# Where the cross-attention mask is added: from ScalarE and TensorE to VectorE in the maximum pass, from TensorE to ScalarE in the second

## The chip, the cores and the metric

The kernel runs on one core of one Trainium2 chip. The metric is the time of one execution on the device in microseconds (us).

## The reference, cut to what matters

A decoder layer over 16 sequences of 256 tokens of width 256: a delta-rule attention block, a cross attention, and a feed-forward block with fake quantization, each behind a layer norm and with a residual. The change touches only the scores of the cross attention, which has 16 heads of width 16 and one mask of 256 x 256 for all sequences and heads:

```
q, k, v = layernorm(x) @ Wq.T, ctx @ Wk.T, ctx @ Wv.T            # split into 16 heads
scores  = q @ k.T / sqrt(16), masked where mask == 0             # [16 sequences, 16 heads, 256, 256]
x       = x + (softmax(scores) @ v) @ Wo.T
```

## The kernel before, in words

The kernel has four phases: `phase_a` (projections and short convolutions), `phase_b` (long convolution and early inverses), `phase_cx` (the rest of the first attention, gates, and the cross attention) and `phase_f` (the feed-forward block). The change lies wholly in `phase_cx`.

`phase_cx` is a software pipeline over the 16 sequences. A hand-written list, `C_ORDER` (L789), names some 250 steps with a stage number. A *turn* goes through this list once; in turn n, a step of stage s works on sequence n - s. Each engine walks the same list and executes its own steps strictly in that order, waiting on semaphores. Five streams of work are so interleaved: stages 0 to 3 of the first attention and its gates, stage 3 of the cross attention's projections, stage 4 its maximum pass, stage 5 its second pass, stages 6 to 8 its output, layer norm and store.

**The maximum pass (stage 4)** finds for each query and head the largest masked score, so that the exponential can be shifted. It has 16 steps (k = 0 to 15), each for one half of the queries and two heads, 128 x 512 scores in the one PSUM bank `psA`:

- `kA` (ScalarE, L1694 to L1701) writes the mask, held twice side by side in `mask_q` as bf16, into `psA` and waits before that for the maximum of step k - 1.
- `sA` (TensorE, L1416 to L1435) waits for the mask and adds the scores of two heads with two matmuls of 96 x 256 that accumulate (`start=False`). Where `masked_by_act` (L1082) is false (the very first step and all of the last sequence) TensorE adds the mask itself, by a matmul of the mask with the identity (L1429).
- `mA` (VectorE, L2134 to L2140) takes both maxima with one `tensor_reduce` of 128 x 512.

After `mA15`, `maxT`, `sh1`, `sh2` and `ld_S` (L1436, L1680, L2141, L1152) turn the maxima, split them into two bf16 rows and store them as two more rows of the stacked queries `Qs`; the second pass subtracts them inside the score matmul.

**The second pass (stage 5)** has 16 steps too, one for each head, 128 x 512 transposed scores (keys by queries) in the one bank `psB`:

- `sB` (TensorE, L1442 to L1459) waits for the exponential of step k - 1 (`pexp_ready`), then writes the mask into the bank by a matmul with the identity (L1454, 512 columns), then adds the scores with two matmuls of 98 x 256 (L1457).
- `eB` (ScalarE, L1693) takes the exponential of the bank into `PT`.
- `pv` (TensorE, L1471) multiplies four heads at a time with V.

The last sequence alternates two banks in the maximum pass and the last two sequences do so in the second pass (`bank_A`, `bank_B`, L1086 and L1091).

Steps of other streams that the prediction names: `proj` and `x1` (L1375, L2079) the first attention's output and residual; `statx`, `rstdx`, `xnx`, `xT`, `xTc`, `qproj`, `qhigh`, `qrest`, `qlow` (L1886, GpSimd, L2131, L1414, L1678, L1397, L1665, L2116, L1861) the layer norm and the query projection, split into three bf16 parts; `ostat` (GpSimd, from L1808), `st8` (L2066), `oT8` (TensorE, L1342) statistics for the output gate; `stats` (GpSimd, from L1772) and `st16` (L1977) those of the kind gates; `w5` (L1556) and `maxT` (L1440), which share a PSUM bank; `xd` (L1551), `OT0` (L1708); `prepare_weights` (L1891), the feed-forward weights' quantization, spread over the `mA` steps of sequence 14.

The mask is prepared once, at `st8` of sequence 0 (L2061), and turned by TensorE into `mask_k` for the second pass.

Of the kernel before, what the change touches and what calls it, by code (L numbers as in the profile page):

```python
# [5 lines left out]
BF16 = mybir.dt.bfloat16  # L6
INT8 = mybir.dt.int8
INT32 = mybir.dt.int32
ALU = mybir.AluOpType
# [739 lines left out]
def weights_T(shared):  # L749
# [39 lines left out]
C_ORDER = [(0, "tt"), (3, "og2"), (3, "oge"), (1, "rv"), (4, "kA1"), (3, "ogs"), (3, "ctxT"), (2, "tT"), (2, "tTc"), (3, "cTc"),  # L789
# [23 lines left out]


def phase_cx(nc, sems, dram, keep, ident, used, early):
    with ExitStack() as ctx:
# [181 lines left out]
        mask_q = xb("mask_q", [P, TT, 2, L], BF16)  # L998
# [83 lines left out]
        def masked_by_act(b, k):  # L1082

            return b < B - 1 and b + k > 0
# [111 lines left out]
        def _(pe):  # L1196
            pe.wait_ge(S_zero, 3)

            def part(op, b):
# [130 lines left out]
                elif op == "oT8":  # L1330
# [3 lines left out]
                    if b == 0:  # L1334

                        pe.wait_ge(prep_step, 6)
                        for t in range(TT):
                            for k in range(TT):
                                nc.tensor.transpose(ps_e_bf[:, 2 * L + k * L + t * P:2 * L + k * L + (t + 1) * P],
                                                    mask_q[:, t, 0, k * P:(k + 1) * P], ident_bf[:])  # L1340
# [75 lines left out]
                elif op[:2] == "sA":  # L1416
# [7 lines left out]
                    if masked_by_act(b, k):  # L1424
                        pe.wait_ge(mask_written, HEAD_STEPS * b + k)
                    else:
                        if b + k > 0:
                            pe.wait_ge(maxed, HEAD_STEPS * b + k - two)
                        nc.tensor.matmul(bank.rearrange("p t q -> p (t q)"), ident_bf[:],  # L1429
                                         mask_q[:, t].rearrange("p s k -> p (s k)"), start=True, stop=False, skip_group_check=True)  # L1430
                    for s in range(2):
                        h = 2 * pair + s
                        last = nc.tensor.matmul(bank[:, s], Qs[slot][0:S_ROWS, h, t * P:(t + 1) * P], Ks[slot][0:S_ROWS, h],  # L1433
                                                start=False, stop=True, skip_group_check=True)
# [7 lines left out]
                elif op[:2] == "sB":  # L1442
# [9 lines left out]
                    if b + k > 0:  # L1452
                        pe.wait_ge(pexp_ready, HEAD_STEPS * b + k - two)
                    nc.tensor.matmul(bank.rearrange("p t q -> p (t q)"), ident_bf[:], mask_k[:].rearrange("p t q -> p (t q)"),  # L1454
# [71 lines left out]
        def _(act):  # L1526
            act.wait_ge(V_set, 1)

            def part(op, b):
# [164 lines left out]
                elif op[:2] == "kA":  # L1694
                    k = int(op[2:])
                    if masked_by_act(b, k):
                        if b == 0 and k == 1:
                            act.wait_ge(prep_step, 6)
# [866 lines left out]
```

## Time and profile before

| what | us |
|---|---|
| median of 3 runs | 1311.63 (1310.03 to 1312.18) |
| the profiled execution's own time | 1311.31 |
| its span in the trace | 1309.5 |
| busy: TensorE, its weight loads | 1086.7, 801.0 |
| busy: VectorE, ScalarE, GpSimd | 958.1, 877.4, 639.4 |

The profiled execution took 1.81 us more than its span. "Busy" counts compute instructions alone; PE is TensorE, PEld its weight loads, DVE VectorE, ACT ScalarE, POOL GpSimd, SP the queue of the DMAs. PEclk is the clock that TensorE was granted, as a share of 2.4 GHz. Matmuls overlap: what one costs the queue is the step from its start to the next one's, not its length. The same holds for VectorE, by some 0.08 us for each instruction. A releaser in brackets is the instruction whose end let a waiting one start. `phase_cx` takes turns of equal length from 481 us on; the turn of 713.0 to 759.6 us stands for them.

### The profile page before, as it was taken

What the parts mean: (1) busy time and instruction counts of PE and PEld (TensorE: products, weight loads), DVE (VectorE), ACT (ScalarE), POOL (GpSimd) and SP (SyncE); (2) the same over time, 40 slices, a digit from 0 to 9 for tenths busy, and PEclk for the clock granted to TensorE, in tenths of its full rate; (3) what the DMA queues carried; (4) which work ended last, traced back from release to release, by engine and by line L of the source; (5) the groups of instructions that cost most, each with busy time, mean ns of one, the idle gap of its engine ahead of it and who ended that gap; (6) DMA issues with size and microseconds to landing.
All of it is one profiled execution on the core that took longest, in us unless ns stands there. A gap on an engine that the chain in (4) does not pass through costs nothing. (4 is left out here: it accounts for less than half of the span.)

```text
span 1309.5 us, 27566 instructions
## 1 busy us (share of the span) xinstructions
PE 1086.7 (83%) x8643; PEld 801.0 (61%) x8643; DVE 958.1 (73%) x2188; ACT 877.4 (67%) x1695; POOL 639.4 (49%) x2360
## 2 busy tenths in 40 slices
PE   5988887685777779999999999999999887876756
PEld 4766666584555556776776676676677655443225
DVE  4988898687666766777877877787787566634985
ACT  4777787432343467878878878887887665444866
POOL 4777775404265355465465556546546643111006
PEclk9988999795566789999999999999999988996989
DMA  5766666546115133333434343343342341205007
GB/s 166 219 186 205 208 198 203 185 88 168 57 57 153 52 103 110 118 100 105 147 110 120 119 122 123 110 135 115 106 146 71 111 118 54 66 34 182 3 1 225
DMA packets 159824, 160.27 MB, mean 122 GB/s; under 512 B 65320, under 2 KB 126656, under 8 KB 159680
## 3 DMA queue, kind: packets, MB, share of 16 engines
q1 hardware_dynamic: 155552, 157.47, 40.0%
q10 hardware_dynamic: 4128, 1.05, 0.4%
q8 instruction: 70, 1.15, 0.4%
q14 instruction: 74, 0.61, 0.2%
HBM read 96.34 MB, written 61.87 MB: 121 GB/s over the span
## 5 line engine op out<-in xcount | busy, mean ns | idle before, releaser
L2140 DVE TENSOR_REDUCE x_maxima<-x_psA 128x2 f32<-128x512 f32 x248 | 170.4, 687 | 93.2 <-PE x_psA L1433 91.3
L1693 ACT ACTIVATE x_PT<-x_psB 128x512 f32<-128x512 f32 x240 | 143.0, 596 | 55.3 <-PE x_psB L1457 51.0
L1700 ACT ACTIVATE x_psA<-x_mask_q 128x512 f32<-128x512 bf16 x239 | 142.3, 595 | 56.2 <-DVE x_maxima L2140 53.1
L314 DVE SCALAR_TENSOR_TENSOR a_conv<-a_ps_proj,taps,a_conv 128x253 f32<-128x253 f32 (+2 forms) x288 | 114.9, 470 | 13.9 <-ACT a_conv L381 13.9
L537 PE MATMUL a_ps_proj<-a_hT,wqkv 128*128 128x256 f32 x384 | 108.4, 433 | 13.9 <-DVE a_conv L314 11.2
L1433 PE MATMUL x_psA<-x_Ks,x_Qs 96*128 96x256 bf16 x496 | 98.2, 280 | 19.8 <-ACT x_psA L1700 19.4
L1454 PE MATMUL x_psB<-x_mask_k,x_ident_bf 128*128 128x512 bf16 x240 | 93.7, 390 | 13.2 <-ACT x_PT L1693 11.1
L537 PEld LDWEIGHTS a_ps_proj<-a_hT,wqkv 128*128 128x128 f32 x384 | 78.7, 215 | 34.3 <-issue 19.4
L1457 PE MATMUL x_psB<-x_Qs,x_Ks 98*128 98x256 bf16 x480 | 93.7, 276 | 0.0
L1861 POOL TENSOR_SCALAR x_parts_q<-x_rest 128x512 bf16<-128x512 f32 x16 | 23.9, 1496 | 115.2 <-DVE x_rest L2116 115.2
L1471 PE MATMUL x_psO<-x_PT,x_V 128*32 128x256 f32 x1024 | 70.6, 394 | 1.1 <-ACT x_PT L1693 1.0
L1433 PEld LDWEIGHTS x_psA<-x_Ks,x_Qs 96*128 96x128 bf16 x496 | 40.6, 99 | 47.0 <-ACT x_psA L1700 26.7
L1457 PEld LDWEIGHTS x_psB<-x_Qs,x_Ks 98*128 98x128 bf16 x480 | 47.8, 100 | 33.9 <-issue 2.4
L2361 POOL TENSOR_TENSOR f_y<-f_y,f_x 128x512 f32<-128x512 f32 x16 | 23.0, 1458 | 86.1 <-DVE f_y L2349 79.4
L381 ACT ACTIVATE a_conv<-a_ps_proj,taps 128x256 f32<-128x256 f32 x96 | 40.4, 477 | 31.0 <-PE a_ps_proj L537 30.7
L1454 PEld LDWEIGHTS x_psB<-x_mask_k,x_ident_bf 128*128 128x128 bf16 x240 | 25.7, 107 | 46.9 <-ACT x_PT L1693 25.1
L1214 PE MATMUL c_ps_gram<-c_keypack 64*128 64x256 f32 x256 | 44.8, 477 | 10.7 <-DVE c_S L1874 6.6
L1861 POOL TENSOR_SCALAR x_parts_k<-x_rest 128x512 bf16<-128x512 f32 x16 | 24.1, 1505 | 44.2 <-DVE x_rest L2116 44.2
L1969 DVE TENSOR_REDUCE c_sums<-c_sq 128x8 f32<-128x512 f32 x64 | 43.0, 676 | 0.0
L1471 PEld LDWEIGHTS x_psO<-x_PT,x_V 128*32 128x32 f32 x1024 | 27.2, 111 | 25.5 <-issue 9.3
L2409 ACT ACTIVATE f_act_gate<-f_ps_gate,f_io_scale_gate 128x512 f32<-128x512 f32 (+1 forms) x48 | 32.4, 685 | 12.4 <-PE f_ps_gate L2449 6.7
L2449 PE MATMUL f_ps_up<-f_xq,shared 128*128 128x512 bf16 (+1 forms) x96 | 30.1, 397 | 12.1 <-DVE f_h L2316 12.1
(387 smaller groups left out, 3241.5 us busy)
## 6 DMA issues: line engine op xcount, KB each, us to landing
scratch_keypack<-a_keypack SPq DMA_DIRECT2D x16, 768.0 KB, 4.5
c_keypack<-scratch_keypack SPq DMA_DIRECT2D x16, 768.0 KB, 4.7
x_Ks<-scratch_k_parts SPq DMA_DIRECT2D x192, 64.0 KB, 2.2
matrix<-scratch_taps_copies SPq DMA_DIRECT2D x32, 256.0 KB, 4.0
scratch_k_parts<-x_parts_k SPq DMA_DIRECT2D x32, 192.0 KB, 2.2
scratch_q_parts<-x_parts_q SPq DMA_DIRECT2D x32, 192.0 KB, 2.2
x_Qs<-scratch_q_parts SPq DMA_DIRECT2D x32, 192.0 KB, 2.9
a_x_in<-in_x SPq DMA_DIRECT2D x16, 256.0 KB, 3.7
```

Source lines behind the costliest of these rows:

```text
L314: nc.vector.scalar_tensor_tensor(acc, ps_proj[PROJ_BANK[p]][:, c, 0:L - j], taps[:, p, c, TAPS - 1 - j:TAPS - j], acc, ALU.mult, ALU.add). ...
L537: last = nc.tensor.matmul(ps_proj[PROJ_BANK[p]][:, o], wqkv[:, p, c, o * P:(o + 1) * P], hT[par][:, c], start=c == 0, stop=c == FC - 1)
L1214: last = nc.tensor.matmul(ps_gram[:, at:at + 2].rearrange("p s n -> p (s n)"), kp[:, 0], kp[:, 1:3].rearrange("p s n -> p (s n)"), start=T ...
L1433: last = nc.tensor.matmul(bank[:, s], Qs[slot][0:S_ROWS, h, t * P:(t + 1) * P], Ks[slot][0:S_ROWS, h], start=False, stop=True, skip_group_ ...
L1454: nc.tensor.matmul(bank.rearrange("p t q -> p (t q)"), ident_bf[:], mask_k[:].rearrange("p t q -> p (t q)"), start=True, stop=False, skip_ ...
L1457: last = nc.tensor.matmul(bank[:, t], Ks[slot][:, k, t * P:(t + 1) * P], Qs[slot][:, k], start=False, stop=True, skip_group_check=True)
L1471: last = nc.tensor.matmul(psO[VW * j:VW * (j + 1), g % 2], V[b % NVB][:, t, h], PT[:, h % (2 * GROUP), t], start=t == 0, stop=t == 1, tile ...
L1693: nc.scalar.activation(PT[:, k % (2 * GROUP)], bank_B(b, k)[0], ACT.Exp, scale=XD ** -0.5).then_inc(pexp_ready, 1)
L1700: nc.scalar.activation(psA[:].rearrange("p t q -> p (t q)"), mask_q[:, k % 2].rearrange("p s k -> p (s k)"), ACT.Copy).then_inc(mask_writt ...
L1861: nc.gpsimd.tensor_scalar(parts[k][:, 1], rest[:], 1.0, None, ALU.mult).then_inc(low_step[k], 1)
L1969: nc.vector.tensor_reduce(sums[:, 2, n], heads(sq[:, (0, 1, 0, 1)[n]]), AX.X, ALU.add).then_inc(sums_ready[n], 1)
L2140: nc.vector.tensor_reduce(maxima[:, t, 2 * pair:2 * pair + 2], bank_A(b, k)[0], AX.X, ALU.max).then_inc(maxed, 1)
```

## The change

1. The maximum pass has no mask in PSUM any more. `sA` overwrites the bank (`start=True`) after waiting for the maximum of step k - 1 alone. `mA` becomes two `tensor_tensor_reduce` instructions, one for each head: (scores + mask) * 1.0 written back into PSUM, and the maximum of it into `maxima`. The mask is a bf16 tile `mask_q` in SBUF, now held once.
2. In the second pass, for sequences 0 to 13 and steps 1 to 15, ScalarE writes the mask (`mask_k`) into `psB` right after the exponential of step k - 1 (new step `kB`), and TensorE's mask matmul goes. `sB` waits for that write. Step 0 and the last two sequences keep the matmul.
3. `kA1` to `kA15` and `kA0` leave `C_ORDER`; `kB1` to `kB15` enter it, each right behind `eB` of the step before. The rest of the order stays.

```diff
-C_ORDER = [(0, "tt"), ..., (1, "rv"), (4, "kA1"), (3, "ogs"), ...
+C_ORDER = [(0, "tt"), ..., (1, "rv"), (3, "ogs"), ...
-           (5, "sB4"), (4, "mA6"), (4, "kA7"), (5, "eB4"), (3, "statx"), (3, "rstdx"), (1, "b0"),
+           (5, "sB4"), (4, "mA6"), (5, "eB4"), (5, "kB5"), (3, "statx"), (3, "rstdx"), (1, "b0"),
...
+LOWEST = -3.0e38
+MASKED_BY_ACT = (1, 2, 3, 4, 5, 6, 7, 8, 9, 10, 11, 12, 13, 14, 15)
...
-        mask_q = xb("mask_q", [P, TT, 2, L], BF16)
+        mask_q = xb("mask_q", [P, TT, L], BF16)
...
-            return b < B - 1 and b + k > 0
+            return b < B - 2 and k in MASKED_BY_ACT
...  sA
-                    if masked_by_act(b, k):
-                        pe.wait_ge(mask_written, HEAD_STEPS * b + k)
-                    else:
-                        if b + k > 0:
-                            pe.wait_ge(maxed, HEAD_STEPS * b + k - two)
-                        nc.tensor.matmul(bank..., ident_bf[:], mask_q[:, t]..., start=True, stop=False, skip_group_check=True)
+                    if b + k > 0:
+                        pe.wait_ge(maxed, HEAD_STEPS * b + k - two)
                     for s in range(2):
                         last = nc.tensor.matmul(bank[:, s], Qs..., Ks...,
-                                                start=False, stop=True, skip_group_check=True)
+                                                start=True, stop=True, skip_group_check=True)
...  sB
-                    if b + k > 0:
-                        pe.wait_ge(pexp_ready, HEAD_STEPS * b + k - two)
-                    nc.tensor.matmul(bank..., ident_bf[:], mask_k[:]..., start=True, stop=False, skip_group_check=True)
+                    if masked_by_act(b, k):
+                        pe.wait_ge(mask_written, len(MASKED_BY_ACT) * b + MASKED_BY_ACT.index(k) + 1)
+                    else:
+                        if b + k > 0:
+                            pe.wait_ge(pexp_ready, HEAD_STEPS * b + k - two)
+                        nc.tensor.matmul(bank..., ident_bf[:], mask_k[:]..., start=True, stop=False, skip_group_check=True)
...  ScalarE
-                elif op[:2] == "kA":
+                elif op[:2] == "kB":
                     if masked_by_act(b, k):
-                        if b == 0 and k == 1:
-                            act.wait_ge(prep_step, 6)
-                        act.wait_ge(maxed, HEAD_STEPS * b + k)
-                        nc.scalar.activation(psA..., mask_q[:, k % 2]..., ACT.Copy).then_inc(mask_written, 1)
+                        act.wait_ge(pexp_ready, HEAD_STEPS * b + k)
+                        nc.scalar.activation(psB..., mask_k[:]..., ACT.Copy).then_inc(mask_written, 1)
...  VectorE
-                        for s in range(2):
-                            nc.vector.tensor_scalar(mask_q[:, :, s], mask_in, 0.0, MASKED, ALU.is_equal, ALU.mult).then_inc(prep_step, 1)
+                        nc.vector.tensor_scalar(mask_q[:], mask_in, 0.0, MASKED, ALU.is_equal, ALU.mult).then_inc(prep_step, 2)
...
-                    nc.vector.tensor_reduce(maxima[:, t, 2 * pair:2 * pair + 2], bank_A(b, k)[0], AX.X, ALU.max).then_inc(maxed, 1)
+                    if b + k == 0:
+                        dve.wait_ge(prep_step, 6)
+                    for s in range(2):
+                        h = 2 * pair + s
+                        last = nc.vector.tensor_tensor_reduce(bank_A(b, k)[0][:, s], bank_A(b, k)[0][:, s], mask_q[:, t], 1.0, LOWEST,
+                                                              ALU.add, ALU.max, maxima[:, t, h:h + 1])
+                    last.then_inc(maxed, 1)
```

## Rows read from the trace of the kernel before

**Rows 1.** The page's costliest groups, by line and engine

```profile
L2140 DVE TENSOR_REDUCE x_maxima<-x_psA 128x2 f32<-128x512 f32 x248 | 170.4, 687 | 93.2 <-PE x_psA L1433 91.3
...
L1693 ACT ACTIVATE x_PT<-x_psB 128x512 f32<-128x512 f32 x240 | 143.0, 596 | 55.3 <-PE x_psB L1457 51.0
...
L1700 ACT ACTIVATE x_psA<-x_mask_q 128x512 f32<-128x512 bf16 x239 | 142.3, 595 | 56.2 <-DVE x_maxima L2140 53.1
```

**Rows 2.** Busy by stretch: length, PE, PEld, DVE, ACT, POOL, clock, DMA, GB/s

```profile
713.00:759.60 46.60, 44.31 (x410) 33.10 (x409) 36.11 (x85) 37.68 (x75) 26.35 (x96) 1.00 0.41 120
...
1040.00:1087.00 47.00, 40.36 (x256) 25.26 (x255) 27.45 (x68) 29.84 (x55) 23.57 (x91) 0.90 0.46 137
```

**Rows 3.** PE's waits in the turn of 713.0: total, times, longest

```profile
PE c_ps_gram L1440 <- ACT c_W L1556: 1.0, 1, 1.0
...
PE x_psB L1454 <- ACT x_PT L1693: 0.6, 1, 0.6
...
PE c_ps_e L1342 <- DVE c_stats L2067: 0.5, 1, 0.5
```

**Rows 4.** Timeline of that turn, second pass: start, length, engine, line

```profile
722.89 0.38 PE L1457 MATMUL x_psB<-x_Qs,x_Ks 98*128 98x256 bf16 x2
...
728.25 0.38 PE L1454 MATMUL x_psB<-x_mask_k,x_ident_bf 128*128 128x512 bf16 x1
...
728.47 0.38 PE L1457 MATMUL x_psB<-x_Qs,x_Ks 98*128 98x256 bf16 x2
...
728.90 0.58 ACT L1693 ACTIVATE x_PT<-x_psB 128x512 f32<-128x512 f32 x1
...
729.84 0.38 PE L1457 MATMUL x_psB<-x_Qs,x_Ks 98*128 98x256 bf16 x2
...
749.08 0.38 PE L1457 MATMUL x_psB<-x_Qs,x_Ks 98*128 98x256 bf16 x2
```

**Rows 5.** Timeline of that turn, DVE: lengths and steps from start to start

```profile
713.37 0.11 DVE L2073 TENSOR_SCALAR c_og<-c_og 128x2 f32<-128x2 f32 x1
...
714.59 0.67 DVE L2140 TENSOR_REDUCE x_maxima<-x_psA 128x2 f32<-128x512 f32 x1
...
715.19 0.67 DVE L1961 TENSOR_REDUCE c_sums<-shared 128x8 f32<-128x512 f32 x1
...
718.12 0.42 DVE L2153 TENSOR_TENSOR x_otok<-c_ps_gram,x_rsum 128x256 f32<-128x256 f32 x1
...
718.47 0.67 DVE L1969 TENSOR_REDUCE c_sums<-c_sq 128x8 f32<-128x512 f32 x1
```

**Rows 6.** Timeline of that turn: DVE from x1 to the normalized x1

```profile
726.99 0.69 DVE L2079 TENSOR_TENSOR c_x<-c_x_in,c_ps_w 128x512 f32<-128x512 f32 x1 [0.44 <-PE c_ps_w L1375]
...
733.74 0.74 DVE L2131 TENSOR_SCALAR x_xn<-c_x,x_mean_var,x_rstd 128x256 f32<-128x256 f32 x2
```

**Rows 7.** Timeline of that turn: the chain through GpSimd to the TensorE wait

```profile
739.23 0.69 DVE L2140 TENSOR_REDUCE x_maxima<-x_psA 128x2 f32<-128x512 f32 x1 [1.25 <-PE x_psA L1433]
...
739.83 0.68 DVE L2116 TENSOR_TENSOR x_rest<-c_ps_gram,x_parts_q 128x512 f32<-128x512 f32 x1
...
740.70 1.50 POOL L1861 TENSOR_SCALAR x_parts_q<-x_rest 128x512 bf16<-128x512 f32 x1 [7.00 <-DVE x_rest L2116]
...
749.88 0.19 DVE L2066 TENSOR_REDUCE c_stats<-c_ostat_v 128x8 f32<-128x32 f32 x1 [1.07 <-POOL c_ostat_v L1825]
...
750.19 0.38 PE L1342 MATMUL c_ps_e<-ident,c_stats 128*8 128x128 f32 x2 [0.51 <-DVE c_stats L2067]
```

**Rows 8.** Timeline, maximum pass of the last sequence

```profile
1138.16 0.38 PE L1429 MATMUL c_ps_w<-x_mask_q,x_ident_bf 128*128 128x512 bf16 x1
```

**Rows 9.** Busy time by stretch, columns as in rows 2

```profile
616.00:620.00 4.00, 3.28 (x22) 2.85 (x22) 2.55 (x7) 2.63 (x7) 3.02 (x10) 1.00 0.03 7
...
1096.00:1100.00 4.00, 1.90 (x11) 0.91 (x10) 3.75 (x7) 0.87 (x2) 0.69 (x1) 1.00 0.34 98
...
1100.00:1104.00 4.00, 3.00 (x12) 1.56 (x12) 3.98 (x8) 2.18 (x4) 0.61 (x3) 0.53 0.01 2
```

More of the change, by code:

```diff
@@ L784 @@
 NVB = 2
-C_ORDER = [(0, "tt"), (3, "og2"), (3, "oge"), (1, "rv"), (4, "kA1"), (3, "ogs"), (3, "ctxT"), (2, "tT"), (2, "tTc"), (3, "cTc"),
[11 rows of a table removed]
+C_ORDER = [(0, "tt"), (3, "og2"), (3, "oge"), (1, "rv"), (3, "ogs"), (3, "ctxT"), (2, "tT"), (2, "tTc"), (3, "cTc"),
[11 rows of a table added]
            (1, "rhs1"), (0, "invr"), (1, "r1"), (4, "sA9"), (3, "ld_K0"), (1, "sqv"), (3, "xT"), (2, "ld_c"), (2, "mixb"), (3, "xTc"),
[1 row of a table removed]
[1 row of a table added]
            (1, "b1"), (1, "w1"), (2, "mixc"), (2, "mix"), (3, "K0st"), (4, "sA10"), (4, "mA10"), (2, "osq"), (0, "invq"), (3, "qrest"),
[6 rows of a table removed]
[6 rows of a table added]
            (5, "sB15"), (5, "eB15"), (2, "og1"), (2, "gelu2"), (4, "sA15"), (5, "pv3"), (0, "invb"), (0, "att1"), (3, "st_qp"), (3, "ld_Q0"),
[1 row of a table removed]
[1 row of a table added]
            (5, "OT1"), (3, "Q0st"), (0, "sums3a"), (3, "vproj"), (3, "vc"), (3, "sA0"), (0, "inve"), (3, "mA0")]
+LOWEST = -3.0e38
+MASKED_BY_ACT = (1, 2, 3, 4, 5, 6, 7, 8, 9, 10, 11, 12, 13, 14, 15)
 def phase_cx(nc, sems, dram, keep, ident, used, early):
@@ L1339, in part @@
                                 nc.tensor.transpose(ps_e_bf[:, 2 * L + k * L + t * P:2 * L + k * L + (t + 1) * P],
-                                                    mask_q[:, t, 0, k * P:(k + 1) * P], ident_bf[:])
+                                                    mask_q[:, t, k * P:(k + 1) * P], ident_bf[:])
                     for t in range(TT):
@@ L1423, in part @@
                         pe.wait_ge(x1_ready, B)
-                    if masked_by_act(b, k):
-                        pe.wait_ge(mask_written, HEAD_STEPS * b + k)
-                    else:
-                        if b + k > 0:
-                            pe.wait_ge(maxed, HEAD_STEPS * b + k - two)
-                        nc.tensor.matmul(bank.rearrange("p t q -> p (t q)"), ident_bf[:],
-                                         mask_q[:, t].rearrange("p s k -> p (s k)"), start=True, stop=False, skip_group_check=True)
+                    if b + k > 0:
+                        pe.wait_ge(maxed, HEAD_STEPS * b + k - two)
                     for s in range(2):
@@ L1451, in part @@
                         pe.wait_ge(delta_ready, B)
-                    if b + k > 0:
-                        pe.wait_ge(pexp_ready, HEAD_STEPS * b + k - two)
-                    nc.tensor.matmul(bank.rearrange("p t q -> p (t q)"), ident_bf[:], mask_k[:].rearrange("p t q -> p (t q)"),
-                                     start=True, stop=False, skip_group_check=True)
+                    if masked_by_act(b, k):
[3 more added lines that the diff above has]
+                            pe.wait_ge(pexp_ready, HEAD_STEPS * b + k - two)
+                        nc.tensor.matmul(bank.rearrange("p t q -> p (t q)"), ident_bf[:], mask_k[:].rearrange("p t q -> p (t q)"),
+                                         start=True, stop=False, skip_group_check=True)
                     for t in range(TT):
@@ L1693, in part @@
                     nc.scalar.activation(PT[:, k % (2 * GROUP)], bank_B(b, k)[0], ACT.Exp, scale=XD ** -0.5).then_inc(pexp_ready, 1)
-                elif op[:2] == "kA":
+                elif op[:2] == "kB":
                     k = int(op[2:])
                     if masked_by_act(b, k):
-                        if b == 0 and k == 1:
-                            act.wait_ge(prep_step, 6)
-                        act.wait_ge(maxed, HEAD_STEPS * b + k)
-                        nc.scalar.activation(psA[:].rearrange("p t q -> p (t q)"), mask_q[:, k % 2].rearrange("p s k -> p (s k)"),
+                        act.wait_ge(pexp_ready, HEAD_STEPS * b + k)
+                        nc.scalar.activation(psB[:].rearrange("p t q -> p (t q)"), mask_k[:].rearrange("p t q -> p (t q)"),
                                              ACT.Copy).then_inc(mask_written, 1)
```

36 rows, old and new, of the table C_ORDER are left out of this document.

## The prediction

> **What bounds the kernel now.** I read the groups by cost first, then busy time by turn, then TensorE's waits inside one turn, then the timeline of that turn. The groups show the three instructions at stake: 248 maxima of 0.687 us on VectorE (8 more of the last sequence read the other bank), 240 exponentials of 0.596 us and 239 mask writes of 0.595 us on ScalarE [rows 1]. Busy time by turn shows which engine is full: in the 46.6 us of a steady turn TensorE is busy 44.31, VectorE 36.11, ScalarE 37.68, GpSimd 26.35 [rows 2]. So TensorE's queue carries the turn, and its few waits say what else does: 1.0 us at `maxT` for a ScalarE copy, 0.6 at one `sB` for the exponential, 0.5 at `oT8` for statistics [rows 3]. The last closes a second loop that runs all the way round: TensorE's `sA10` releases `mA10`, which VectorE awaited for 1.25 us, then `qrest`, then GpSimd's `qlow` from 740.70 and the output statistics, `st8` at 749.88, and `oT8` at 750.19 [rows 7]; from there TensorE runs through its queue to the next `sA10`. Whatever lengthens that loop lengthens the turn. There are twelve such turns (481 to about 1040 us), and the mask work of 14 sequences lies in or just around them.
>
> **The change, part by part, with one steady turn as the unit.**
>
> *Mask matmuls leave TensorE.* The step from the start of the mask matmul to that of the score matmuls is 728.47 - 728.25 = 0.22 us [rows 4]. 15 of them go in a turn: 3.3 us of queue time.
>
> *Their place is taken by a ScalarE write in the loop of `psB`.* From score matmuls to exponential takes 728.90 - 728.47 = 0.43 us [rows 4], the exponential 0.60 [rows 1]. Before, TensorE could then add mask and scores. Now `kB` must wait for the end of `eB` (its own engine's semaphore), takes 0.60 [rows 1], and only then may the score matmuls start. With some 0.04 us for each of the two handovers, the shortest step from score matmuls to score matmuls is 0.43 + 0.60 + 0.04 + 0.60 + 0.04 = 1.70 us. In the turn shown there are sixteen starts of L1457; the fifteen gaps between them reach from 1.37 us (728.47 to 729.84) to 4.1, and seven are shorter than 1.70: those that end at steps 2, 4, 5, 6, 8, 12 and 14, the first at 722.89, the last at 749.08 [rows 4]. These seven sum to 10.56 us and must grow to 11.90: +1.34. The other eight lose their 0.22 (one of them, at 1.83 us, only 0.13): -1.67. TensorE's queue thus gains 0.33 us of the 3.3; the rest turns into waits for `kB`. Behind a waiting `sB` stand the transposes, projections and solves of the other streams, since the queue is in order.
>
> *ScalarE's load.* 15 writes come for 16 that went, so 0.6 us less. But a `kB` may stand ahead of something urgent: before `xTc` and before `qhigh` one now lies where a `kA` lay after or elsewhere; I take 0.1 us for both. `kA`'s own waits go, 56.2 us over the kernel [rows 1]; they blocked ScalarE's queue, but what came next in it mostly waited for TensorE anyway.
>
> *The loop of `psA`* loses a 0.60 us write and a handover and gains the longer maximum, below. It gets shorter, and VectorE's waits for `sA` can absorb some of that. Cost nothing; the cover is those waits (93.2 us in all [rows 1]).
>
> *The maximum on VectorE.* Before: one reduction, 715.19 - 714.59 = 0.60 us from start to start. Now two instructions that stream 256 elements each. No row shows a `tensor_tensor_reduce`. From below, the two-operand instruction of 256 elements from PSUM takes 718.47 - 718.12 = 0.35 us from start to start. From above I take 0.60, the whole old reduction of twice the elements. I choose 0.45: the two-operand row plus the smallest instruction, 0.11 us, for getting the maximum out [rows 5]. A step of `mA` then costs 0.90 for 0.60: +0.30 us, 4.8 a turn on an engine with 10 us to spare (+0.10 and +0.60 at the ends).
>
> The Trainium skill ("VectorE: DVE Perf Modes", section on two Vector instructions with no wait between them) says that an operation which also writes out its accumulator is two instructions, the main one and an accumulator read. It speaks against this change: four instructions for one. No row here shows one; the page gives no price, and if two tiny instructions are meant, the sum above already has them.
>
> *Where VectorE's addition meets the loop.* Two places. From `x1` at 726.99 to `xnx` at 733.74 VectorE runs almost without a pause, with three maxima in between [rows 6]. `x1` itself comes 0.50 us earlier (gaps 15, 1, 2, 3: -0.22, -0.22, +0.16, -0.22), the maxima add 0.90, so `xT` comes about 0.2 late; the wait of `sB8` right behind it (net +0.08 since the turn's start for gaps 15 to 8) swallows most of that, so +0.1. Then `mA10` and `qrest`, directly in the loop [rows 7]: +0.30. With ScalarE's 0.1, the loop grows by 0.5 us a turn. TensorE's own queue at `oT8` then is no later than that.
>
> *Outside the steady turns.* The last sequence's maximum pass had TensorE add each mask by L1429, 0.38 us long like L1454 [rows 4, 8], so again 0.22 us of queue. 16 x 0.22 = 3.5 us go, in a stretch where TensorE is full; the longer maxima give part of it back. I take -2. The turn with the weight quantization has VectorE as its tight engine, but loses a handover through ScalarE at each step: 0. One mask preparation less, once: 0, as VectorE waits in that turn.
>
> *Sum:* 12 x 0.5 - 2 = +4 us on 1311.31, the profiled execution's own time (its span is 1309.5, and it lies 0.3 under the median of 1311.63): about **1315**.
>
> **The rivals.**
>
> *The turn shortens (faster).* Mechanism: without `kA`'s waits ScalarE reaches its exponentials earlier, so the waits of `sB` on them [rows 3] vanish, the maxima cost 0.35 each and hide in VectorE's idle time, and the loop through GpSimd moves forward with TensorE. Then the turn gains 0.33 + 0.6 = 0.9 us: 12 x -0.9 - 3.5 = -14, **1297**. It decides once the seven short gaps need less than 1.65 us, or the maxima less than about 0.35. For it: TensorE is the fullest engine and loses work. Against it: the seven gaps, and `mA10` in the loop.
>
> *The new reduction is dear (slower).* At 0.60 us each, the three maxima before `xnx` add 1.8, `xT` comes 0.9 late, `mA10` adds 0.6: 1.5 a turn, 12 x 1.5 - 1 = +17, **1329**. It decides above about 0.5 us, where VectorE's chain and no longer `kB` sets `xT`.
>
> *Nothing moves.* The two sides cancel within the noise, or the steps do not bind where I think: **1311.6**.
>
> *TensorE's clock falls (slower).* Short waits now lie between its matmuls. In 1096 to 1100 us TensorE was busy 1.90 of 4 us, and the clock granted next was 0.53, 1.2 GHz for nearly all of that stretch [rows 9]. The turn of 1040 to 1087, busy 40.36 of 47, ran at 0.90 in the mean [rows 2]. If the steady turns ran so, a tenth of some 41 us would be lost in each: 12 x 4 = 49, **1360**. Against it: at 616 to 620 it was busy 3.28 of 4 and kept 1.00 [rows 9], and no wait that I expect exceeds 0.5 us. The Trainium skill ("TensorE: Matmul & The Clock Gate", Part 1) has the throttled state as the default, which activity releases; the rows agree, and I expect about 88% activity.
>
> **How the numbers follow.** A difference under 0.2% (2.6 us) can't be told from none. The forecast, 0.50 (its own range 1310 to 1319: 0.30 of it slower, 0.18 same, 0.02 faster); the shorter turn 0.25 (0.22 faster, 0.03 same); the dear reduction 0.15; nothing moves 0.05; the clock 0.05. Together slower 0.50, same 0.26, faster 0.24. The range, 1302 to 1327, takes in most of both neighbours and leaves out their far ends and the clock.
>
> **What would show it.** Right: steady turns of 47.1 us for 46.6; TensorE busy about 41 us in them and waiting for L1700's successor at steps 2, 4, 5, 6, 8, 12, 14, with 1.7 us between those score matmuls; new VectorE instructions 0.45 us apart and VectorE at about 41 us a turn; granted clock 1.00. Wrong: score matmuls closer than 1.6 us or no TensorE wait on the mask write; a turn under 46.4 us; VectorE waiting no longer for `sA10`, with steps of 0.55 us or more; or a granted clock under 1.00 between 500 and 990 us.

## The result and the profile after

The changed kernel takes 1348.38 us (median of 4 runs, 1340.92 to 1349.23) against 1310.83 us of the kernel before in the same session: ratio 1.0278, 95% interval 1.0252 to 1.0303, so 2.8% or some 37 us slower. The forecast was 1315, its range ended at 1327. The profiled execution took 1347.73 us, its span 1345.6 us, the mean granted clock was 0.876 (0.908 before).

The page of the changed kernel, its costliest groups; they answer to [rows 1] and [rows 4]:

```profile
span 1345.6 us, 27831 instructions
...
PE 1093.3 (81%) x8397; PEld 798.4 (59%) x8416; DVE 990.7 (74%) x2955; ACT 876.5 (65%) x1666; POOL 636.2 (47%) x2360
...
L2142 DVE CUSTOM_DVE_ANT_0 x_psA<-x_psA,x_mask_q 128x256 f32<-128x256 f32 x496 | 201.6, 448 | 110.1 <-PE x_psA L1431 108.9
...
L1694 ACT ACTIVATE x_PT<-x_psB 128x512 f32<-128x512 f32 x240 | 143.3, 597 | 111.8 <-PE x_psB L1458 110.1
...
L1458 PE MATMUL x_psB<-x_Qs,x_Ks 98*128 98x256 bf16 x480 | 103.2, 300 | 51.6 <-ACT x_psB L1699 50.3
...
L1699 ACT ACTIVATE x_psB<-x_mask_k 128x512 f32<-128x512 bf16 x210 | 126.3, 601 | 6.7
...
L2142 DVE DVE_READ_ACCUMULATOR2_ANT x_maxima<- 128x1 f32 x512 | 72.3, 141 | 0.0
```

Each head's maximum is two instructions on VectorE, the main one and an accumulator read. L1458, the second pass's score matmuls, waited 50.3 us in all for L1699, ScalarE's mask write.

Busy time of three turns, columns as in [rows 2]; turns are cut here from one `maxT` to the next:

```profile
565.51:613.22 47.71, 42.76 (x393) 31.58 (x395) 38.10 (x131) 38.15 (x74) 25.43 (x93) 1.00 0.37 112
...
613.22:663.29 50.07, 45.58 (x393) 32.70 (x395) 38.49 (x133) 38.34 (x74) 28.25 (x100) 0.93 0.38 112
...
713.16:763.39 50.23, 45.81 (x393) 32.63 (x394) 38.25 (x132) 38.28 (x74) 27.12 (x99) 0.93 0.38 111
```

This is the view that decides. In the eleven turns from 515.37 to 1063.72 us only one, the first row, ran at clock 1.00, and it took 47.71 us. The other ten took 49.87 to 50.23: nine at 0.93, and the last at 0.86, though that one executes fewer matmuls (345 for 393), as the first attention's early stages have run out. The kernel before took 46.59 at 1.00, and 44.26 for the last of the eleven. TensorE's waits in one of the slow turns (716.7 to 766.5 us), as [rows 3]:

```profile
PE x_psB L1458 <- ACT x_psB L1699: 2.8, 7, 1.1
...
PE c_ps_gram L1438 <- ACT c_W L1557: 1.0, 1, 1.0
```

And where in that turn the clock fell, in stretches of 4 us:

```profile
728.00:732.00 4.00, 4.00 (x27) 3.45 (x25) 3.12 (x11) 1.72 (x4) 2.65 (x2) 1.00 0.04 12
732.00:736.00 4.00, 3.04 (x27) 1.84 (x27) 3.64 (x20) 3.65 (x9) 1.68 (x9) 1.00 0.73 221
736.00:740.00 4.00, 3.99 (x32) 1.79 (x33) 2.67 (x11) 2.04 (x6) 1.17 (x6) 0.57 0.00 0
...
748.00:752.00 4.00, 2.88 (x24) 2.44 (x24) 3.31 (x10) 3.88 (x9) 3.40 (x11) 1.00 0.34 101
752.00:756.00 4.00, 3.55 (x22) 1.83 (x26) 2.88 (x10) 3.14 (x6) 2.66 (x13) 0.64 0.39 101
```

Behind the stretch with the closely spaced steps 4, 5 and 6 (PE busy 3.04 of 4), and again behind 748 to 752 (2.88), where steps 11 and 12 wait, the granted clock is 0.57 and 0.64, which means 1.2 GHz for most of the stretch. Other slow turns have one fall that lasts about twice as long, some of them at steps 5 and 6 and some at steps 11 and 12, as in the turn from 613.22:

```profile
650.00:654.00 4.00, 2.94 (x12) 1.60 (x13) 2.59 (x7) 3.00 (x6) 2.64 (x14) 0.59 0.52 141
654.00:658.00 4.00, 4.00 (x28) 1.71 (x27) 2.13 (x10) 2.40 (x5) 3.09 (x13) 0.55 0.00 0
```

The steps themselves were as predicted. Second pass, from score matmuls to score matmuls 734.12 - 732.40 = 1.72 us:

```profile
732.40 0.39 PE L1458 MATMUL x_psB<-x_Qs,x_Ks 98*128 98x256 bf16 x2 [0.31 <-ACT x_psB L1699]
...
732.83 0.60 ACT L1694 ACTIVATE x_PT<-x_psB 128x512 f32<-128x512 f32 x1 [0.19 <-PE x_psB L1458]
...
733.46 0.60 ACT L1699 ACTIVATE x_psB<-x_mask_k 128x512 f32<-128x512 bf16 x1
...
734.12 0.39 PE L1458 MATMUL x_psB<-x_Qs,x_Ks 98*128 98x256 bf16 x2 [0.39 <-ACT x_psB L1699]
```

Maximum pass, VectorE, one step of `mA` and what follows it:

```profile
737.80 0.43 DVE L2142 CUSTOM_DVE_ANT_0 x_psA<-x_psA,x_mask_q 128x256 f32<-128x256 f32 x1 [0.49 <-PE x_psA L1431]
...
738.15 0.14 DVE L2142 DVE_READ_ACCUMULATOR2_ANT x_maxima<- 128x1 f32 x1
...
738.15 0.47 DVE L2142 CUSTOM_DVE_ANT_0 x_psA<-x_psA,x_mask_q 128x256 f32<-128x256 f32 x1
...
738.53 0.73 DVE L2129 TENSOR_SCALAR x_xn<-c_x,x_mean_var,x_rstd 128x256 f32<-128x256 f32 x2
```

The two heads start 0.35 us apart and the next instruction 0.38 later: 0.73 us for a step that took 0.60 before.

**Where the time went, by the two profiled executions.** Their spans differ by 1345.6 - 1309.5 = 36.1 us. The eleven turns that follow the second `maxT` took 548.35 us for 510.56: +37.8. The next three took 124.84 for 118.63: +6.2, at clocks of 0.79, 0.74 and 0.90 for 0.89, 0.85 and 1.00. The rest to the end differs by 0.2. The second `maxT` itself came 7.7 us earlier (515.37 for 523.08): the first one already came 9.3 us earlier (468.74 for 478.00), nearly all that runs ahead of it is code that the change does not touch, and in the traces of the experiments it lies anywhere from 464.3 to 474.5, so I read nothing into it. In the middle of `phase_cx` the price is thus 37.8 / 11 = 3.4 us a turn. It is the price of a usual slow turn too (50.0 for 46.6); the one turn at full clock lost 1.1, and the last of the eleven 5.9. The experiments split these 3.4 us.

### The profile page after: what moved, and what is told of

The parts are those of the page before. It is cut to its first block and busy times, and to the rows that moved or that the text cites. A ratio compares the mean times of both kernels' runs of the same rounds, so it can differ in the third digit from the quotient of the medians.

```text
span 1345.6 us, 27831 instructions
## 1 busy us (share of the span) xinstructions
PE 1093.3 (81%) x8397; PEld 798.4 (59%) x8416; DVE 990.7 (74%) x2955; ACT 876.5 (65%) x1666; POOL 636.2 (47%) x2360
## 5 line engine op out<-in xcount | busy, mean ns | idle before, releaser
L2142 DVE CUSTOM_DVE_ANT_0 x_psA<-x_psA,x_mask_q 128x256 f32<-128x256 f32 x496 | 201.6, 448 | 110.1 <-PE x_psA L1431 108.9
L1694 ACT ACTIVATE x_PT<-x_psB 128x512 f32<-128x512 f32 x240 | 143.3, 597 | 111.8 <-PE x_psB L1458 110.1
L1458 PE MATMUL x_psB<-x_Qs,x_Ks 98*128 98x256 bf16 x480 | 103.2, 300 | 51.6 <-ACT x_psB L1699 50.3
L1699 ACT ACTIVATE x_psB<-x_mask_k 128x512 f32<-128x512 bf16 x210 | 126.3, 601 | 6.7
L1431 PE MATMUL x_psA<-x_Ks,x_Qs 96*128 96x256 bf16 x496 | 103.9, 294 | 13.7 <-DVE x_maxima L2142 13.5
L1458 PEld LDWEIGHTS x_psB<-x_Qs,x_Ks 98*128 98x128 bf16 x480 | 36.4, 102 | 111.7 <-ACT x_psB L1699 93.0
L1472 PE MATMUL x_psO<-x_PT,x_V 128*32 128x256 f32 x1024 | 86.3, 465 | 1.5 <-ACT x_PT L1694 1.5
L2142 DVE DVE_READ_ACCUMULATOR2_ANT x_maxima<- 128x1 f32 x512 | 72.3, 141 | 0.0
L1431 PEld LDWEIGHTS x_psA<-x_Ks,x_Qs 96*128 96x128 bf16 x496 | 44.9, 103 | 39.1 <-DVE x_maxima L2142 15.0
L1217 PEld LDWEIGHTS c_ps_gram<-c_keypack 64*128 64x128 f32 x256 | 28.5, 238 | 22.8 <-issue 12.7
L334 DVE SCALAR_TENSOR_TENSOR a_shortT<-a_vT,a_short_taps,a_shortT 128x255 f32<-128x255 f32 (+2 forms) x96 | 39.1, 476 | 1.0 <-ACT a_shortT L419 1.0
```

The source lines that it names most:

```text
L1217: last = nc.tensor.matmul(ps_gram[:, at:at + 2].rearrange("p s n -> p (s n)"), kp[:, 0], kp[:, 1:3].rearrange("p s n -> p (s n)"), start=T ...
L1458: last = nc.tensor.matmul(bank[:, t], Ks[slot][:, k, t * P:(t + 1) * P], Qs[slot][:, k], start=False, stop=True, skip_group_check=True)
L1472: last = nc.tensor.matmul(psO[VW * j:VW * (j + 1), g % 2], V[b % NVB][:, t, h], PT[:, h % (2 * GROUP), t], start=t == 0, stop=t == 1, tile ...
L1694: nc.scalar.activation(PT[:, k % (2 * GROUP)], bank_B(b, k)[0], ACT.Exp, scale=XD ** -0.5).then_inc(pexp_ready, 1)
L1699: nc.scalar.activation(psB[:].rearrange("p t q -> p (t q)"), mask_k[:].rearrange("p t q -> p (t q)"), ACT.Copy).then_inc(mask_written, 1)
L2142: last = nc.vector.tensor_tensor_reduce(bank_A(b, k)[0][:, s], bank_A(b, k)[0][:, s], mask_q[:, t], 1.0, LOWEST, ALU.add, ALU.max, maxima[ ...
```

## Experiments

Each is the changed kernel with the edit shown, unless said otherwise. Ratios are to the kernel before in the same session. "Turn" is the usual time from `maxT` to `maxT` in the middle of `phase_cx`; it was 46.59 us before.

### The maximum pass alone

```diff
-MASKED_BY_ACT = (1, 2, 3, 4, 5, 6, 7, 8, 9, 10, 11, 12, 13, 14, 15)
+MASKED_BY_ACT = ()
```

> The maximum pass alone is changed (VectorE adds its masks, no kA); in the second pass TensorE keeps its mask matmul and ScalarE writes nothing. Theory W (the loss lies in the mask write's place in the loop of psB, by its waits and by TensorE's clock that falls behind them): steady turns of 46.5 to 46.8 us, granted clock 1.00 in them, 1307 to 1312 us. Rival V (VectorE's four instructions for one, and what stands behind them, cost it): the turn stays above 48 us and the time at 1325 or more.

Measured: 1305.83 us, ratio 0.9998 (0.9972 to 1.0024). One turn, and TensorE's wait for the statistics at `oT8` in a turn:

```profile
654.07:700.96 46.89, 44.43 (x408) 33.10 (x409) 37.80 (x131) 29.66 (x59) 26.36 (x96) 1.00 0.40 119
...
PE c_ps_e L1345 <- DVE c_stats L2065: 0.8, 1, 0.8
```

A turn of 46.9 us at clock 1.00, a tenth above the expected range: the half of the change that sits on VectorE costs 0.3 us a turn and no measurable time. Rival V is out. Those 0.3 are about where the prediction had put them: the gap that ends at step 8, behind `xnx`, grew from 1.54 to 1.70 us, and the wait at `oT8` from 0.5 [rows 3] to 0.8.

### The mask write where there was room, and where there was none

Two runs: in one ScalarE writes for the steps whose gap (the time from the score matmuls of the step before to its own) was longer than the floor of 1.70 us, in the other for those whose gap was shorter. The first added line is the one run, the second the other:

```diff
-MASKED_BY_ACT = (1, 2, 3, 4, 5, 6, 7, 8, 9, 10, 11, 12, 13, 14, 15)
+MASKED_BY_ACT = (1, 3, 7, 9, 10, 11, 13, 15)
+MASKED_BY_ACT = (2, 4, 5, 6, 8, 12, 14)
```

> ScalarE writes the second pass's mask only for the eight steps whose gap before was longer than the 1.70 us floor (1, 3, 7, 9, 10, 11, 13, 15); TensorE adds the others. Theory W: eight matmuls of 0.22 us leave, no wait comes, clock 1.00, turn 45.9 us, about 1300 us. Rival C (fewer matmul columns let the clock fall, whatever the waits are): granted clock 0.93 to 0.97 in the steady turns and over 1320 us. Rival V as in the run with the maximum pass alone: over 1325.

> ScalarE writes the mask only for the seven steps whose gap was shorter than the floor (2, 4, 5, 6, 8, 12, 14). Theory W: it carries all of the loss; by the waits alone 7 gaps grow by 1.34 us in sum and the time is about 1324; with the clock falling behind them, turns of 49 to 50 us, clock 0.93 to 0.95, 1340 to 1350. Rivals C and V: no more than half of the loss (C) since the matmuls are back, 1330 or less with clock near 1.00.

Long gaps: 1302.06 us, ratio 0.9956 (0.9933 to 0.9979), clock 1.00. A turn, and then ScalarE and the score matmuls around step 11 of a turn:

```profile
610.83:657.39 46.56, 43.51 (x401) 32.22 (x401) 37.75 (x131) 34.15 (x67) 26.34 (x95) 1.00 0.39 120
...
689.50 1.69 ACT L1552 ACTIVATE c_solve<-X 32x256 f32<-32x256 f32 x4
...
691.21 0.60 ACT L1694 ACTIVATE x_PT<-x_psB 128x512 f32<-128x512 f32 x1
...
691.84 0.60 ACT L1699 ACTIVATE x_psB<-x_mask_k 128x512 f32<-128x512 bf16 x1
...
692.50 0.39 PE L1458 MATMUL x_psB<-x_Qs,x_Ks 98*128 98x256 bf16 x2 [0.47 <-ACT x_psB L1699]
```

It is faster than the kernel before, and neither the clock nor VectorE stood against it. But I had expected 45.9 us: the eight matmuls that left, 8 x 0.22 = 1.76 us, bought only 0.3 us against the 46.9 with the maximum pass alone. The timeline says where part of it stayed: at step 11 the exponential (L1694) starts only behind four copies of the solve (L1552, to 691.19), and the mask write (L1699) behind that. The gap grew from 2.84 to 3.38 us. A write there had room in `psB`'s own loop but not in ScalarE's queue.

Short gaps: 1344.91 us, ratio 1.0303 (1.0261 to 1.0346). Seven writes carry all of the loss. Three of its turns:

```profile
667.80:716.35 48.55, 44.09 (x402) 32.39 (x403) 38.12 (x131) 33.56 (x66) 26.47 (x96) 1.00 0.38 116
...
716.35:766.05 49.70, 45.41 (x402) 32.88 (x403) 38.21 (x131) 33.68 (x66) 26.45 (x96) 0.97 0.37 112
...
915.48:966.46 50.98, 46.81 (x401) 33.90 (x402) 38.22 (x131) 33.68 (x66) 26.46 (x96) 0.93 0.36 110
```

The steps are the same in each of them. At 1.00 the turn takes 48.55 us, at 0.97 (one slow stretch, in 739 to 743 us) 49.70, at 0.93 (one twice as long, in 937 to 944) 50.98. So in this kernel the seven writes cost 48.55 - 46.9 = 1.65 us a turn by their waits, the short slow stretch another 1.2 and the long one 2.4. Step 3, which has no write, was late as well (4.57 us for 4.11), and ScalarE's queue shows why: the copy L1712, which TensorE's output projection L1498 awaits, now stands behind the write for step 2.

```profile
680.53 0.60 ACT L1699 ACTIVATE x_psB<-x_mask_k 128x512 f32<-128x512 bf16 x1
...
681.07 0.58 ACT L1712 ACTIVATE x_ofT<-c_ps_gram 128x512 f32<-128x512 f32 x1
...
681.79 1.97 PE L1498 MATMUL c_ps_gram<-x_wo,x_ofT 128*128 128x256 f32 x8 [0.21 <-ACT x_ofT L1712]
```

### TensorE's work given back, behind the wait

```diff
                         pe.wait_ge(mask_written, ...)
+                        nc.tensor.matmul(bank..., zero_bf[:], mask_k[:]..., start=False, stop=False, skip_group_check=True)
```

`zero_bf`, a tile of zeros, is filled once at the start (not shown).

> The whole change, and behind each wait for the mask write TensorE adds a matmul of 512 columns with weights of zero, which adds nothing to the bank but gives back the work that the change took away; the floor of a step grows from 1.71 to 1.93 us. Theory clock (a falling clock costs some 3 us of each turn): granted clock back at or near 1.00, turn 48.5 to 49.5 us, 1330 to 1345, no slower than the changed kernel though it does more. Rival, waits alone: 15 times 0.22 us more in each turn, turn 51.5 to 53 us, 1365 to 1385 us.

Measured: 1380.08 us, ratio 1.0569 (1.0528 to 1.0611). Two turns:

```profile
578.25:628.12 49.87, 45.61 (x409) 33.06 (x410) 38.00 (x129) 38.45 (x74) 25.29 (x95) 1.00 0.36 107
...
682.03:736.07 54.04, 49.90 (x408) 35.21 (x409) 38.30 (x131) 38.53 (x74) 26.39 (x96) 0.91 0.34 104
```

My clock theory in this form fell: with 15 more matmuls of 512 columns nine of the eleven turns ran at 0.90 to 0.97, no better than 0.93 on the whole. The time is the one that the rival gave, but not for its reason: the full turn at 1.00 took 49.87 us, and the clock brought the others to as much as 54.04. A mere number of columns is not what had been missing. The waits were still empty, and they had stayed as long as they were (2.9 us in that turn, 1.1 the longest). These matmuls have weights of zero; whether others would have acted otherwise was not tried.

### Three waits in a row, and four apart

Two runs again, one for each line:

```diff
-MASKED_BY_ACT = (1, 2, 3, 4, 5, 6, 7, 8, 9, 10, 11, 12, 13, 14, 15)
+MASKED_BY_ACT = (4, 5, 6)
+MASKED_BY_ACT = (2, 8, 12, 14)
```

> ScalarE writes the mask for steps 4, 5 and 6 alone, three short gaps in a row. By the floor of 1.70 us three gaps grow by 0.24, 0.34 and 0.1 to 0.26: waits alone give 47.6 to 47.8 us a turn, 1315 to 1322 us. Theory clock-by-cluster (it is this row of waits that lets the granted clock fall once a turn): 0.96 to 0.97 in the turn and 48.7 to 49 us, 1328 to 1335. Rival: the clock holds at 1.00 and falls only with all seven waits.

> ScalarE writes the mask for steps 2, 8, 12 and 14 alone, the four short gaps that stand apart. The gaps grow by 0.17, 0, 0.41 and 0.17 us, and step 3's by the 0.46 that its copy of the sixth stage's output stands behind the write: 47.2 to 47.9 us a turn. Theory clock-by-cluster: clock 1.00, 1310 to 1320 us. Rival (a single wait is enough, as before 752 to 756 us in the changed kernel): clock 0.96 to 0.97, 48.5 to 49 us a turn, 1328 us or more.

Three in a row: 1336.51 us, ratio 1.0261 (1.0213 to 1.0309). Three of its turns, and TensorE's waits for the write in the last of them:

```profile
566.96:614.60 47.64, 44.24 (x406) 32.81 (x407) 37.95 (x131) 31.46 (x62) 26.32 (x96) 1.00 0.38 112
...
762.56:811.30 48.74, 45.50 (x406) 33.46 (x407) 38.06 (x131) 31.57 (x62) 26.33 (x96) 0.96 0.37 115
...
712.47:762.56 50.09, 46.96 (x405) 34.26 (x406) 38.10 (x131) 31.58 (x62) 26.32 (x96) 0.93 0.36 112
...
PE x_psB L1458 <- ACT x_psB L1699: 0.7, 2, 0.4
```

And the clock in that last turn, whose steps 4, 5 and 6 start at 731.51, 733.23 and 735.66 us:

```profile
732.00:736.00 4.00, 3.61 (x26) 2.52 (x25) 3.42 (x20) 3.30 (x7) 2.48 (x12) 0.66 0.44 139
736.00:740.00 4.00, 4.00 (x31) 1.65 (x30) 1.87 (x8) 1.14 (x3) 0.51 (x3) 0.50 0.02 4
```

Four apart: 1309.96 us, ratio 1.0067 (1.0040 to 1.0095). A turn, and its waits for the write:

```profile
653.53:701.14 47.61, 44.28 (x404) 32.67 (x405) 37.81 (x131) 31.70 (x63) 26.22 (x96) 1.00 0.38 118
...
PE x_psB L1458 <- ACT x_psB L1699: 1.6, 3, 1.1
```

This is the clearest pair of the study. The four writes that stand apart make TensorE wait longer (1.6 us a turn, one wait being 1.1) and leave the clock at 1.00 in all of the eleven turns; they cost 47.6 - 46.9 = 0.7 us. (Behind these, in the turn with the weight quantization, the clock was 0.83 for 0.93 in the run with the maximum pass alone.) The three in a row make it wait 0.9 us in their one turn at 1.00, never over 0.4, cost 0.74 us there (47.64), and bring the clock down in all the others, to 0.93 in five of them. Three writes do nearly the whole damage of fifteen, more than the 1328 to 1335 us that I had expected. In the turn whose clock is shown two of the three waits, 0.31 and 0.39 us, had passed when the clock fell; the third did not come any more, as TensorE itself was late.

### All but these three

```diff
+MASKED_BY_ACT = (1, 2, 3, 7, 8, 9, 10, 11, 12, 13, 14, 15)
```

> The changed kernel, where TensorE adds the mask of steps 4, 5 and 6 again; ScalarE still writes twelve. Theory cluster (these three waits in a row bring the clock down, and it then falls once more behind steps 11 to 14): at least one of the two slow stretches of each turn goes, clock 0.97 to 1.00, 47.0 to 48.5 us a turn, 1312 to 1330 us. Rival (any two thirds of the waits are enough): clock 0.93 as in the changed kernel and 49 us or more, 1338 us or more.

Measured: 1316.16 us, ratio 1.0095 (1.0072 to 1.0118). A usual turn, and one of the two full turns at clock 1.00:

```profile
605.69:653.68 47.99, 44.35 (x396) 32.58 (x397) 38.09 (x133) 36.48 (x71) 27.14 (x99) 0.96 0.39 117
...
750.00:796.77 46.77, 42.84 (x396) 31.86 (x397) 37.54 (x129) 36.32 (x71) 24.96 (x93) 1.00 0.40 120
```

With 12 of 15 writes kept, two thirds of the loss are gone. The slow stretch behind steps 4 to 6 no longer appears in the turn from 605.69 us; one is left behind step 12 (clock 0.76 from 641 to 645 us, 0.81 to 649), and costs 1.2 us a turn (47.99 for 46.80). At that step the run with four apart had the same write and the same wait of 1.1 us, but none at step 11 before it or at step 13 behind, and kept its clock: so it is not the one wait. Whether steps 4 to 6 are also a bad place by themselves, without three writes in a row, no run separates.

### The waits filled

The bank `psO` is free at steps 4 to 6 and at 12, and what is written there is overwritten before it is read.

```diff
+                        if k in (4, 12):
+                            if 2 * b + (k == 12): pe.wait_ge(OT_ready, 2 * b + (k == 12))
+                        for _ in range({4: 2, 5: 2, 6: 2, 12: 4}.get(k, 0)):
+                            nc.tensor.matmul(psO[:, 0], ident_bf[:], mask_k[:, 0], start=True, stop=True, skip_group_check=True)
                         pe.wait_ge(mask_written, ...)
```

> The whole change, and TensorE does idle work inside its waits: in front of the wait for the mask write it issues matmuls of 256 columns into the bank of the second pass's output, free there and overwritten later (two each at steps 4, 5 and 6, four at step 12, 0.11 us each). They fit into waits that are there anyway, so the step's floor stays 1.71 us. Theory idle (the clock falls because TensorE stands idle several times in a row, and it costs 2.4 us of each turn): the granted clock rises to 0.97 or more, turns of 47.7 to 48.9 us, 1312 to 1330 us, faster than the changed kernel though it executes more. Rival wait (the semaphore waits themselves, or the wide change of the order, bring it down): clock 0.93 as before, 50 us or more a turn, 1345 us or more.

Measured: 1316.0 us, ratio 1.0125 (1.0070 to 1.0179). A turn, and its waits for the write:

```profile
652.84:700.53 47.69, 43.91 (x402) 32.26 (x404) 38.05 (x131) 38.13 (x74) 26.12 (x96) 1.00 0.39 118
...
PE x_psB L1462 <- ACT x_psB L1703: 2.1, 7, 0.6
```

All eleven turns ran at clock 1.00, ten of them in 47.69 to 47.75 us: to 0.02 us the one turn that the changed kernel had at full clock (47.71). TensorE executes ten matmuls more in each turn, whose results nobody reads, and the kernel is about 20 us faster than the changed one ((1.0278 - 1.0125) x 1311). This also splits the price by measurement: the same eleven turns took 510.56 us before, 522.43 here and 548.35 in the changed kernel, so 11.9 us for the longer steps and 25.9 for the clock. The last of the eleven took 45.44 here for 50.19 there. The cure is not complete: of the four executions two took 1311 us, the profiled one among them, and two 1321 and 1323, at mean clocks of 0.900 and 0.896 for 0.907 and 0.910, so in those the clock probably fell in some turns; no trace of them is kept. The matmuls behind the wait had three times as many columns (15 x 512 for 10 x 256) and did not help; these lie inside the waits. They also have other weights (the identity, not zeros), which no run separates from their place. Of the theories I had, only the idle one fits all runs: the clock fell because TensorE stood idle, shortly but repeatedly.

### What the reduction's two instructions cost, and what the removed write had cost

The maximum pass alone (`MASKED_BY_ACT = ()`), with the one reduction of before:

```diff
-                    for s in range(2):
-                        last = nc.vector.tensor_tensor_reduce(...)
+                    last = nc.vector.tensor_reduce(maxima[:, t, 2 * pair:2 * pair + 2], bank_A(b, k)[0], AX.X, ALU.max)
```

It leaves the mask out of the maxima, so the exponentials are shifted by the largest score of all keys and not of the unmasked ones.

> The maximum pass alone is changed, and VectorE takes both maxima with the one reduction of before, without a mask (the mask is left out of the maxima; ScalarE writes none). It isolates what VectorE's four instructions for one cost. In the run with the maximum pass alone the turn was 46.9 us. Theory loop: the 0.13 us by which each step on VectorE is longer (0.73 for 0.60) comes back where it lay in the chain (steps 6 to 8 and 10), 46.5 to 46.6 us a turn, the value of before, so that the removed ScalarE write is worth nothing. Rival: without its mask write the maximum pass lets the turn fall below that of before, 46.2 us or less.

Measured: 1290.61 us, ratio 0.9909 (0.9881 to 0.9937). A turn:

```profile
603.61:650.15 46.54, 44.24 (x408) 33.18 (x409) 35.99 (x83) 29.62 (x59) 26.19 (x96) 1.00 0.40 121
```

The turn is 46.54 us, that of before: VectorE's share is 46.9 - 46.54 = 0.36 us a turn, and the ScalarE write that left the maximum pass was worth nothing in the turn. Yet the kernel is 0.9% faster. Its last four intervals of `maxT` took 158.3 us for 162.9, so 4.6 us come from the sequences at the end, where TensorE no longer adds the mask; in the run with the maximum pass alone, whose maxima are the longer ones, they took 162.6. The clock differed there as well (0.96 for 0.93 in one of the four), so the split is argued and not shown. The rest of the 12 us I can't place. As a shift changes no softmax while its exponentials stay in range, leaving the mask out of the maxima is the cheaper form where scores allow it; how far they may spread was not tried.

### The loop, and other ways to use the gain

```diff
+MASKED_BY_ACT = (1, 3, 7, 9, 13, 15)
```

> As the run with the eight long gaps, without the writes for steps 10 and 11 (steps 1, 3, 7, 9, 13, 15 remain). In that run step 11's gap had grown from 2.83 to 3.38 us, as its exponential and its write both stand behind ScalarE's copies of the solve, and TensorE still waited 0.4 us for the statistics. Theory loop (the chain through GpSimd to the statistics sets the turn): no change, 46.5 to 46.7 us a turn, 1298 to 1303 us. Rival queue (TensorE's own queue sets it): the 0.6 us come back, 46.0 to 46.1 us a turn, 1293 to 1297 us.

Measured: 1301.19 us, ratio 0.9995 (0.9976 to 1.0015). A turn, and the wait at `oT8`:

```profile
602.19:648.62 46.43, 43.54 (x402) 32.39 (x403) 37.62 (x131) 33.12 (x65) 26.20 (x95) 1.00 0.40 121
...
PE c_ps_e L1345 <- DVE c_stats L2065: 1.0, 1, 1.0
```

Step 11's gap was 2.84 us again, and the wait for the statistics grew by 0.6 us, from 0.4 to 1.0: what the queue gained, the loop through GpSimd took. The queue's theory wanted 46.0 to 46.1 us and is out; the loop's wanted 46.5 to 46.7, and the same kernel with all eight long gaps took 46.56 in one session and 46.40 in another, so 46.43 is no change. The other run is the kernel before with its whole maximum pass, and the same six writes added to the second pass, each behind the exponential of the step before:

```diff
-           (5, "sB0"), (5, "eB0"), (1, "sums0"), ...
+           (5, "sB0"), (5, "eB0"), (5, "kB1"), (1, "sums0"), ...
...
+        def masked_B(b, k):
+            return b < B - 2 and k in (1, 3, 7, 9, 13, 15)
```

> The maximum pass as before the change (ScalarE writes its mask, one reduction on VectorE), and ScalarE also writes the second pass's mask for steps 1, 3, 7, 9, 13, 15. Theory loop: VectorE's longer maxima cost 0.3 us a turn in the run with the maximum pass alone, so this is the better one of the two: 46.0 to 46.3 us a turn, 1295 to 1300 us. Rival S (ScalarE, at 37.7 + 6 x 0.6 = 41.3 us a turn, gets late with its exponentials): 46.6 us or more, 1303 us or more, and TensorE's waits for ScalarE above 2 us a turn.

Measured: 1305.36 us, ratio 1.0023 (0.9996 to 1.0050). A turn:

```profile
609.85:656.24 46.39, 43.95 (x402) 32.21 (x403) 35.70 (x83) 40.98 (x81) 26.35 (x95) 1.00 0.40 121
```

It gave 46.4 us a turn, between the two theories, and no gain in time: theory loop had wanted 1295 to 1300 us. ScalarE at 41 us a turn does not break it.

### The fastest version again

> The same kernel as the run with the eight long gaps (steps 1, 3, 7, 9, 10, 11, 13, 15), timed again in more rounds, as the fastest version so far. If its gain is real: 0.994 to 0.998 of before. Rival: it was the draw of that chip, 0.998 to 1.002.

Measured: 1298.79 us, ratio 0.9953 (0.9931 to 0.9974), after 0.9956 in the first session. With the write at the eight long gaps alone the change is a gain of 0.5%: faster than the kernel before and 3.2% faster than the changed one (0.9953 / 1.0278 = 0.968).

## Why the prediction was wrong

**Direction right, size wrong by 33 us.** Step by step:

- **The new step of the second pass**, 1.70 us: measured 1.71 and 1.72. Right, and so were the seven steps where it binds.
- **Seven short gaps, +1.34 us.** In the changed kernel's turn at full clock they went from 10.56 to 12.15: +1.59, as step 6 took 1.90. Nearly right.
- **"The other eight lose their 0.22 (...): -1.67."** Measured 22.71 to 22.13 us: -0.58. This is the first step that failed. I had asked of a write only whether `psB`'s loop had room for it, and gave ScalarE's queue 0.1 us a turn. At step 3 the copy that TensorE awaits stood behind a write (+0.24 instead of -0.22), at step 11 exponential and write both stood behind the solve's copies (+0.54 instead of -0.22), and step 10 came at +0.09. All fifteen gaps together came out at +1.01 instead of -0.33.
- **VectorE, 0.45 us for an instruction pair, +0.30 a step.** Measured 0.35 and 0.38, +0.13 a step, 38 us busy a turn where 41 were forecast. Too high, though inside the bounds (0.35 to 0.60). That it would cost some tenths in the loop was right: 0.3 us a turn, against 0.4 without ScalarE's share, though partly by luck: each step grew by less than half of what was put in for it.
- **The loop grows by 0.5 us a turn.** At full clock it grew by 47.71 - 46.59 = 1.12: 0.3 for VectorE and 0.8 for the waits. The twelve turns would then have cost 13 us where the sum had 6, and the filled kernel, at ratio 1.0125, lost 16. (The working of the 0.5 has a slip as well: 0.90 - 0.50 is 0.40, not the 0.2 us by which `xT` was to come late. It decided nothing.)
- **"TensorE's clock falls", chance 0.05.** This is the step that decided: the sum had no term for the clock, and the clock cost 25.9 us in the eleven turns. Among the signs of being wrong was "a granted clock under 1.00 between 500 and 990 us", and it came. I had dismissed it because "no wait that I expect exceeds 0.5 us" and because one stretch of the old trace with PE busy 3.28 of 4 had kept 1.00 [rows 9]. The first reason is refuted by the run with three writes in a row, whose waits for the write never exceeded 0.4 us. It is true that one wait came to 1.1 us, against my expectation, but the run with four apart had that one too and kept its clock. Its price was 50.0 - 47.7 = 2.3 us of each turn; I had put 4 on the whole, from a turn at 0.90. The last three long turns, where I expected part of a gain of 2 us, lost 6.2 at lower clocks.

So the 3.4 us of a slow turn are about 0.3 for VectorE, 0.8 for the waits net of the matmuls that left, and 2.3 for the clock. The direction was right for reasons that hold, but they explain only about a third of the loss (11.9 of the 37.8 us in the eleven turns). Eleven turns at 3.4 and the 6.2 at the end are 44 us, and the start gave 8 back in the profiled pair.

The Trainium skill describes such a fall ("TensorE: Matmul & The Clock Gate", section "A second HAM failure mode: psum-queue depth-cycling") for a kernel that cycles through PSUM banks: TensorE "micro-idles between MM groups frequently enough that HAM oscillates". HAM is its name for what gates TensorE's clock. This case's traces agree: waits of 0.31 and 0.39 us in two successive steps, and a granted clock of 0.66 and 0.50 in the two stretches of 4 us around and behind them. I had cited that page for the released state alone.

## What to carry to other kernels

When an edit takes work from a nearly full TensorE and puts short waits in its place, price its clock, not only the waits: here a net 0.8 us of waits cost 2.3 us more. Look at how closely the waits follow each other rather than at the longest one, and leave such steps as they were, or put the missing work into the wait itself and not behind it. And ask of a moved instruction what room it has in its new engine's queue, apart from the room in its buffer's loop: a write with plenty of slack at its bank still delayed a copy that TensorE awaited.

## What the runs showed that I had not expected

- Identical turns of one execution differ by 2.4 us through the clock alone (48.55 at 1.00, 50.98 at 0.93), and come in groups: the run with the short gaps kept 1.00 for two turns, fell for one, and had 0.93 in the last three full ones. Which turn falls I can't tell from the trace, and no run tried it.
- Matmuls whose results nobody reads, issued inside the waits, brought TensorE's turns in the profiled execution from a clock of 0.93 to 1.00 and made the kernel about 20 us faster, while three times as many columns behind the wait left the clock low and made it 38 us slower (ratio 1.0569 for 1.0278).
- `tensor_tensor_reduce` on 128 x 256 from PSUM is a pair of instructions whose accumulator read, 0.14 us long, mostly overlaps: the pair costs 0.35 to 0.38 us from start to start, hardly more than the 0.35 of a plain two-operand instruction of that size [rows 5].
